# Two layers of a gated cross-attention block with experts: eight padding transfers moved behind a pair of small ones, and one PSUM bank cleared by matrix products instead of a memset

## The reference, cut to what matters

```python
q = _heads(x @ Wq + bq); k = _heads(x @ Wk + bk); v = _heads(x @ Wv + bv)      # H = 16 heads of 8
att = jnp.einsum('bhqd,bhkd->bhqk', q, k) * scale
att = jnp.where(causal[None, None], att, -jnp.inf)
y = jnp.einsum('bhqk,bhkd->bhqd', jax.nn.softmax(att, axis=-1), v)
qc = _heads(x @ Wcq + bcq); kc = _heads(cross_input @ Wck + bck); vc = _heads(cross_input @ Wcv + bcv)
attc = jnp.einsum('bhqd,bhkd->bhqk', qc, kc) * scale                           # 512 context rows
y = y + jnp.einsum('bhqk,bhkd->bhqd', jax.nn.softmax(attc, axis=-1), vc)
return y @ Wp + bp
```

## Time and profile before

| | |
|---|---|
| Time, median of 3 runs | 333.73 us (333.17 to 334.24) |
| Profiled execution, span | 337.6 us |
| TensorE busy | 312.9 us, 93% |
| VectorE, ScalarE, GpSimd busy | 65%, 57%, 34% |
| TensorE's share of the chain that ended last | 73% |
| Mean granted TensorE clock | 0.995 |

### The profile page before, as it was taken

The page is one execution under the profiler, slowest core; times in us unless marked ns, Lnnn a source line. Parts: engine busy times, 40 slices in busy tenths (PEclk is TensorE's granted clock), DMA queues, the critical chain, the costliest instruction groups (busy, mean ns, idle before and its releaser), DMA issues.

```text
span 337.6 us, 7474 instructions
## 1 busy us (share of the span) xinstructions
PE 312.9 (93%) x2891; PEld 189.6 (56%) x2891; DVE 220.8 (65%) x532; ACT 194.1 (57%) x410; POOL 115.7 (34%) x200
## 2 busy tenths in 40 slices
PE   8998969989999999899977999999996899999995
PEld 3545733334443434344666677777794357776665
DVE  4998798888989889676242052333321956779665
ACT  3468588978888889787266733323336265512221
POOL 6476732327334333231775003444442211110000
PEclk9999999999999999999997999999999999999999
DMA  7855995940437006240441580000002200000101
GB/s 174 199 110 160 175 213 132 209 90 10 153 110 209 5 5 188 70 124 2 109 157 35 133 212 10 21 18 19 22 12 70 71 0 2 1 2 0 31 3 31
DMA packets 35827, 27.83 MB, mean 82 GB/s; under 512 B 5627, under 2 KB 33070, under 8 KB 35792
## 3 DMA queue, kind: packets, MB, share of 16 engines
q1 hardware_dynamic: 33965, 25.04, 29.7%
q0 software_dynamic: 1280, 1.88, 1.7%
q10 hardware_dynamic: 547, 0.44, 0.5%
HBM read 11.89 MB, written 5.26 MB: 51 GB/s over the span
## 4 chain that ended last, share of the span: by engine, by line
PE 73%; ACT 7%; DVE 6%; issue 5%; POOL 5%; DMA 2%; SPq 0%; DVEq 0%; POOLq 0%; ACTq 0%
PE psum L1682 11%; PE psum L1876 11%; PE psum L1957 8%; PE psum L1624 5%; PE psum L1648 5%; PE psum L1945 4%; PE psum L1864 4%; ACT qk_r L948 3%; PE psum L1814 2%; POOL rows_in L797 2%; PE psum L1651 2%; PE psum L2060 2%; PE psum L2052 1%; PE psum L1575 1%; PE psum L1869 1%
## 5 line engine op out<-in xcount | busy, mean ns | idle before, releaser
L1213 DVE TENSOR_REDUCE nmax<-psum 128x2 f32<-128x1024 f32 (+2 forms) x88 | 102.0, 1216 | 11.6 <-PE psum L1624 10.3
L948 ACT ACTIVATE parts<-psum 128x512 f32<-128x512 f32 (+1 forms) x88 | 45.2, 566 | 8.6 <-PE psum L1648 7.7
L1876 PE MATMUL psum<-p_more,kcat 128*128 128x320 f32 (+2 forms) x160 | 40.2, 396 | 0.9 <-DVE p_more L1346 0.7
L819 POOL DMA_INDIRECT rows_back<-qcat,back_at x24 | 22.9, 952 | 50.3 <-ACT qcat L981 43.1
L1876 PEld LDWEIGHTS psum<-p_more,kcat 128*128 128x128 f32 x160 | 26.1, 190 | 9.1 <-issue 0.9
L1350 DVE TENSOR_TENSOR qcat<-psum,qk_r 128x320 f32<-128x320 f32 (+2 forms) x40 | 16.6, 422 | 22.1 <-ACT qk_r L989 13.5
L989 ACT ACTIVATE qk_r<-psum 128x320 f32<-128x320 f32 (+2 forms) x40 | 15.2, 384 | 24.5 <-PE psum L1876 21.5
L1682 PE MATMUL psum<-parts,v_aug 128*18 128x256 f32 (+1 forms) x352 | 28.5, 369 | 0.0
L1957 PE MATMUL psum<-h_t,kcat 128*128 128x512 f32 x60 | 28.1, 594 | 0.0
L1682 PE MATMUL psum<-qk_r,v_aug 128*18 128x256 f32 (+1 forms) x160 | 27.4, 373 | 0.0
L1648 PE MATMUL psum<-qcat,kcat 64*128 64x256 bf16 x256 | 24.7, 271 | 1.9 <-ACT p_more L948 0.8
(11 more groups left out here) (249 smaller groups left out, 630.4 us busy)
## 6 DMA issues: line engine op xcount, KB each, us to landing
kcat<-parts SPq DMA_DIRECT2D x18, 192.0 KB, 3.8
qcat<-parts SPq DMA_DIRECT2D x21, 128.0 KB, 3.6
kcat<-ones_b SPq DMA_DIRECT2D x8, 192.0 KB, 4.6
kcat<-in_L_ffn_wi_gate_dram SPq DMA_DIRECT2D x6, 256.0 KB, 4.5
kcat<-in_L_ffn_wi_up_dram SPq DMA_DIRECT2D x6, 256.0 KB, 4.8
kcat<-in_L_ffn_wo_dram SPq DMA_DIRECT2D x6, 256.0 KB, 5.0
parts<-in_L_ffn_w_dram SPq DMA_DIRECT2D x3, 512.0 KB, 5.6
rows_in<-zeros SPq DMA_DIRECT2D x1, 1290.0 KB, 5.7
```

Of the source, the lines that this page charges most:

```text
L819: pool.indirect_dma_start(out=rows_back[:, :], out_offset=bass.IndirectOffsetOnAxis(ap=back_at[0:m, e, t:t + 1], axis=0), in_=eo[0:m, e % ...
L948: act.activation(p_slots[u % NPT][:, 0:w], s2_bank(s2_place[u])[:, 0:w], ACT.Exp, scale=SCALE).then_inc(p_in, 1)
L1213: dve.tensor_reduce(dst[:, :, n * g:n * (g + 1)], src.rearrange("p (r q k) -> p r q k", r=PAR, q=n), AX.X, ALU.max, negate=True).then_inc( ...
L1876: ins = pe.matmul(gate_up_bank(i, m)[:, 0:end - first], w_t[e][:, m, f * P:(f + 1) * P], xs_t[:, e % 2, first:end], start=True, stop=True)
```

## The change

In the issue order of SyncE `pad(2)` and `pad(3)` go from behind the maximum rows of part 1 to behind those of part 2, ahead of `load_late()`. The memset of bank 7 by VectorE goes. In its place TensorE does one product of zeros over the whole bank (128 x 128 with 128 x 512, bf16) behind `scores2` in each of the six steps of quad 0, and waits, before the first, for the projection that last used the bank. `values` no longer waits for `o_clear`, except past `TAIL`, where it counts one less. Two idle products of zeros are added behind the context transpose of batch 3.

```diff
+        N_CLEAR = 1
@@ sync: the loop over parts
                 if n == 1:
                     lay_out_batch(3)
+                if n == 2:
                     pad(2)
                     pad(3)
-                if n == 2:
                     load_late()
@@ vector
             split(SPLIT_DVE, 0, QW, False)
-            wait_taken(dve, max(j for j in range(len(jobs)) if job_bank[j] == O_BANK))
-            dve.memset(bank(O_BANK), 0.0).then_inc(o_clear, 1)
@@ tensor
             UNREAD_AFTER = {("ct", 0): (2, 7), ("bias", 0): (2, 7), ("k", 0): (5, 7), ("ct", 1): (2, 2), ("ck", 1): (12, 3),
-                            ("xt", 2): (9, 3)}
+                            ("xt", 2): (9, 3),
+                            ("ct", 3): (2, 7)}
@@ values(n, r)
-                    pe.wait_ge(o_clear, 1 + int(n > TAIL))
+                    if n > TAIL:
+                        pe.wait_ge(o_clear, 1)
@@ the loop over steps, behind scores2(step)
+                if n == 0:
+                    if step == 0:
+                        wait_taken(pe, max(j for j in range(len(jobs)) if job_bank[j] == O_BANK))
+                    unread_zeros(N_CLEAR, O_BANK)
```

## The result

The changed kernel takes 331.9 us (median of 4 runs, 331.56 to 333.15) against 333.57 us for the kernel before beside it (4 runs, 333.17 to 334.24): ratio 0.9949, 95% interval 0.9924 to 0.9973. That is 1.67 us or 0.5% faster; 332.2 was predicted. Timed once more, last, beside 16 runs of the kernel before: 332.03 us (11 runs, 331.67 to 333.64) against 334.76, ratio 0.9933, interval 0.9907 to 0.9958.

The account below looks back on a forecast made before the run. TensorE holds most of the chain, with a DMA wait at step 24. The terms -1.56 + 0 + 0 + 0 take 333.73 to 332.2 us, 0.47% faster; range 331.0 to 333.9.

Parts of the forecast that it names:

- The wait's worth: First layer's pass 2, step 24: TensorE's scores wait for part 2's second maximum row; without that DMA, 1.56 us less.
- Rows issued right behind the copy: SyncE, part 2: rows issued from 65.45, the second at about 66.2, landing at about 68.5, before 69.93.
- Batch 2's paddings: Moved behind the rows, issued by 69.6, landed by 74.7; part 4's first unit wants them at 76.1: 1.4 us to spare.
- Late loads: Ten loads for GpSimd's `add_bias`, last issued at 77.3, landing 79.1 against a limit of 79.4: cost 0, upper end 0.2.
- the warning: The late loads' cover before step 36 was not called safe: once gone, every microsecond of delay is one of TensorE's.
- Zero products: TensorE, quad 0 and behind the context transpose: 0.216 us each fits the idle gaps, 0.08 to spare at the narrowest; cost 0.
- Weight loads: Skill's rule, set aside: each zero product would cost 0.1 us more, overfill two 0.30 us gaps by 0.01, sum -1.54.
- The memset: VectorE at 19.55, 0.48 us: its first maximum could start at most 0.04 earlier, then TensorE idles 0.80 us; gain 0.
- Rival (D): More than summed: a TensorE stall near 180 us falls elsewhere, up to 3.8 us more go, 328.4 us; chance 0.06.
- the profiled execution's excess: The profiled span, put at 3.9 us above the median of the runs; this difference was carried over unchanged.

Follow-up runs that it names:

- the second profile before: The kernel before, unchanged, timed and profiled again: 335.09 us, ratio to itself 1.0019.
- the clearing alone: The changed kernel with the eight paddings back in their old place, keeping the dropped memset and the zero products: 334.65 us, ratio 1.0.
- the run with small transfers: Changed kernel with 13 transfers of 512 bytes ahead of part 2's rows and batch 3's paddings behind part 3's rows: 336.38 us, one run.
- the loads ahead: The changed kernel with the ten late loads issued ahead of the eight paddings, all behind part 2's rows: 333.77 us, ratio 0.9978.
- the move alone: The kernel before with only the eight paddings moved; memset kept, no zero products added: 331.81 us, ratio 0.9917.
- longer wait: The kernel before with four more 192 KB transfers ahead of the eight paddings: 336.38 us, ratio 1.0075.

## Why the prediction was right

- **The wait's worth** was put at 1.56 us. From step 6 to step 24 it is 1.55 less in the profiles compared, and 1.68 and 2.06 less than in the second profile before and in the clearing alone (22.77 and 23.15 us), since the rows' issue varies from 67.19 to 67.81 by execution. In runs at full clock (0.997 and up), 333.81 - 331.95 = 1.86 us. The 0.65 us from ScalarE's start to the scores came as in the earlier trace rows. The scores came at 69.51, not 69.93, because that execution started 0.43 earlier.
- **Rows issued right behind the copy** and landed in time: right. The estimate of 68.5 for the second one rests on 2.3 us; 1.92 was measured in the run with small transfers.
- **Batch 2's paddings** keep their cover: right, no wait at 75.8. The size, 1.4 us, was too small, since it rests on the longest landing, 5.7 us. With the loads ahead, the last of the four was issued 4.27 us later against step 24 (73.90 - 69.92, was 69.22 - 69.51) and the unit came 1.07 us later against it, so the cover is some 3.2 us, an estimate from these rows.
- **Late loads**: landing was put at 79.1 against a limit of 79.4. The last went out at 76.63 instead of 77.3, and landing was faster than the middle I took. Of the changed kernel's two profiles the first has no wait in GpSimd, the second 0.31 us (start at 78.46, last mask done 83.53, TensorE wants it at about 84.2); the move alone has 0.65 us, with the last load issued at 76.84 and there 1.9 us later. None reaches TensorE; 0.3 to 0.9 us of cover are left. The cost of 0 was right, and so was the warning. The 2.0 us that the Trainium skill gives ("DMA: Bandwidth & Descriptors", Anatomy of one DMA), measured for transfers issued from GpSimd, agree with the 1.9 measured here for one issued from SyncE.
- **Zero products**: 0, right; steps 1 to 6 keep their times, as seen above. The two behind the context transpose took the idle time there from 0.88 to 0.44 us. But in quad 0 two sizes were off and happened to offset each other. A product was put at 0.216 us, and it takes 0.42 us of the stream: the unit used to follow the scores after 0.23 us, in the kernel before,

```profile
43.62 0.39 PE L1648 MATMUL psum<-qcat,kcat 64*128 64x256 bf16 x4 [0.36 <-ACT p_more L948]
43.85 0.38 PE L1624 MATMUL psum<-kcat,qcat 64*128 64x512 bf16 x2
```

  and now follows after 0.65 (43.19 to 43.84, above), so it comes to VectorE 0.42 us later instead of 0.2, at no cost that shows. And the narrowest gap was put at 0.30 us, from modelled ends, where it is 0.46: in the kernel before the last unit of quad 0 starts 0.68 us ahead of the scores (48.17 to 48.85), and where nothing holds them the scores follow such a unit after 0.22 (48.98 to 49.20, with two products a step). In the changed kernel they follow after 0.25 (48.17 to 48.42). So the margin was 0.03 to 0.04 us, not 0.08.
- **Weight loads.** The prediction set aside the rule of the Trainium skill ("TensorE: Matmul & The Clock Gate", Part 3, Packing small matmuls), by which a weight load overlaps running products only if its row group differs. TensorE's weight load of the unit behind a zero product, in the changed kernel:

```profile
43.83 0.10 PEld L1624 LDWEIGHTS psum<-kcat,qcat 64*128 64x128 bf16 x2 [0.23 <-issue]
```

  It starts 0.31 us behind the start of the zero product and 0.01 ahead of the unit's products, at 43.84. The zero product's own load starts at 43.51, 0.01 ahead of it too. In the kernel before, without the zero product, the unit's load starts at 43.74, 0.11 ahead of its products. So between these 64-row and 128-row products the trace agrees with the rule, and among twelve equal products it doesn't. By these rows the 0.2 us above 0.216 are two loads of 0.1 us, one on each side; that is an estimate, since the ends of products are modelled.
- **The memset**: gain 0, right; VectorE's first maximum waits for TensorE in its stead, and the next group of maxima starts at 28.48, the old 28.91 less the 0.43 of start-up.

```profile
19.48 8.36 DVE L1212 TENSOR_REDUCE nmax<-psum 128x2 f32<-128x1024 f32 x7 [0.47 <-PE psum L1624]
```

- **Rival (D)**, the stall near 180 us, did not go by the change: the kernel before runs without it too. The 1.80 us by which its 24 transposes were too long were the clock, 0.50 at 182 to 184 us. To leave the profiled execution's excess on both sides was therefore right. Its size was not 3.9 us, though: that compares a span with a time, and the time is 1.75 us more than the span. The excess was 5.6 us over the median of 333.73, and the sum doesn't depend on it.
- **What the sum lacked.** A wait was priced at its length. In about 3 in 10 executions of the kernel before the mean granted clock was 0.993 or less, and such runs take 335.81 - 333.81 = 2.0 us more. In the one profile of it that is such a run, the fall stands behind the wait of step 24 and costs 1.45 us; the rest of the 2.0 may be late falls. That makes up to 0.31 x 2.0 = 0.6 us of the mean, which the changed kernel gains on top. Over all runs the means are 334.67 and 332.30 us, 2.4 apart, against 1.86 at full clock. The ratios of the later samples that take the wait away and add no product (0.9917, 0.9914, 0.9944 and 0.9933) lie at or below the first (0.9949) and the predicted 332.2 / 333.73 = 0.9954, as that would have it; but their intervals overlap, and the forecast was met by the first sample, which had too few runs to show this term.

## What to carry to other kernels

A transfer on which the critical engine waits goes ahead of bulk transfers that are wanted later, on the same queue: here an issue 1.77 us and more too late and a landing 1.0 to 1.4 us longer cost 1.55 to 2.06 us, and half of the move would have been enough. Before such a move, work out the latest time that costs nothing for all that falls behind: 79.4 us by arithmetic and 79.5 to 79.6 by experiment. A gap that one added product just fills is measured between starts, not from modelled ends: the margin here was 0.03 us. And look at the mean granted clock of every run, not only of the profiled one, since a single profile can miss what a third of the runs do.

## What the runs showed of the hardware

- The clock of TensorE fell to its lower level for some 3.4 us behind waits of 1.80 and 2.30 us in an otherwise full stream (granted clock 0.54 and 0.61 in the windows from 72 to 76 us; 0.75, 0.50 and 0.89 from 72 to 78), at a price of 1.45 and 1.51 us. Behind 1.68 and 2.18 us at step 24 and 1.80 us at step 36 in other profiles it did not, and with a wait of 4.77 us it fell during the wait. One program does both: 33 of 106 runs had a mean of 0.993 or less.
- The size of a transfer hardly shows in what its issue takes of SyncE's queue: 13 of 512 bytes took 6.60 us, most of them 0.43 each and one 1.09; a padding of 192 KB takes 0.60. Single issues took 1.28 (changed kernel) and 2.19 us (longer wait) for no reason that the traces show.
- A small DMA is there 1.9 us behind its issue with few or no data in front (1.92 in the run with small transfers, 1.9 in the move alone), and 2.9 to 3.4 us behind the eight paddings. In the run with the longer wait, behind the paddings and the issue of 2.19 us, it was 1.95.
- One product of 128 rows between 64-row ones took 0.42 us of TensorE's stream, and 0.216 in a row of its like.
- One execution can hold 2 us waits that no other has: the first profile before was 5.8 us longer than the median run's span, by three waits of 1.5 to 2.0 us and a fall of the clock.
